# A quantised feed-forward whose up product runs on integers, with the token scale applied behind it

## The chip, the cores and the metric

The kernel runs on one core of a Trainium2 chip. The metric is the device time of one execution in microseconds (us). Three executions of the kernel before took 1745.68, 1744.78 and 1759.41 us; the median is 1745.68 us. Everything is computed in one launch. The engines are named as in the profile: PE is TensorE, DVE is VectorE, ACT is ScalarE, POOL is GpSimd, SP is the queue that only issues transfers.

## The reference

Eight sequences of 512 tokens with 512 features pass through four residual layers: cross attention with 16 heads, a mixture of experts, a second cross attention without projections, and a feed-forward with quantised operands. The change touches the last two layers only:

```python
def act_quant(x):
    scale = 127.0 / jnp.clip(jnp.max(jnp.abs(x), axis=-1, keepdims=True), 1e-05)
    return jnp.clip(jnp.round(x * scale), -128, 127) / scale
def weight_quant(w):
    scale = 1.0 / jnp.clip(jnp.mean(jnp.abs(w)), 1e-05)
    return jnp.clip(jnp.round(w * scale), -1, 1) / scale
...
h = bit_linear(x, w1)                       # act_quant(x) @ weight_quant(w1).T, 512 -> 2048
h = depthwise_conv1d(h.transpose(0, 2, 1), conv_w, conv_b)   # three taps along the tokens
h = jax.nn.silu(h.transpose(0, 2, 1))
return bit_linear(h, w2)                    # act_quant(h) @ weight_quant(w2).T, 2048 -> 512
```

The scale of `act_quant` is one number for each token (row), so it can be taken out of the matrix product and applied to its result.

## The kernel before

The program is four stages, one after the other: `attention`, `experts`, `fuse` and `ffn`. The first two end at about 1134 us of the profiled span and are not touched.

**fuse** handles the second attention. It runs in steps `s` from -1 to 8, a software pipeline over the eight sequences (batches, `B` = 8, `TB` = 4 tiles of 128 tokens each). In step `s`, `front` combines the expert outputs for batch s+1 into `x1`, `mid` runs the attention of batch s and writes `x3`, and `back` quantises batch s-1: ACT normalises into `xq`, DVE takes the row maximum `am`, ACT rounds by adding `MAGIC`, DVE multiplies back by the scale (`dequantise`, L1704), PE transposes (`out_transposes`, L1806), ACT copies to `xdT_out` (`copy_out`, L1641), and SP writes that to the scratch `xdT_d` (`store`). In its last steps the stage reads batch 0 back, and POOL splits it into a high and a low part (`first_parts`, L1603 and L1606), so that PE can compute the first four tiles of the feed-forward (`first_ups`, L1817) inside the stage.

**ffn** runs in steps `s` from -1 to 9. In step `s`, `f1` computes the 16 tiles `m` (128 hidden features by 512 tokens each) of batch s, `quant` finds and applies the token scales of batch s-1's hidden values, and `f2` is the down product of batch s-2. For one tile: `up(m)` on PE multiplies w1q with the two parts of `xdT` into one of four PSUM banks (`RING` = 4; L2145, eight matmuls); ACT writes the middle tap and the bias into the tile of `h` (L2009); DVE adds the two outer taps, reading the PSUM bank and `h` (`taps`, L2049 and L2052, signal `conv_done`); ACT applies SiLU (L1988). `half_max` (L2060) takes the maximum over eight tiles after m = 9 and over the other eight at the step's end; PE transposes the maxima (L2155), DVE makes scales of them (`token_scales`, L2065 to L2072), PE spreads them to a row (`scale_row`, L2161), ACT copies it to `srow` (L2002). Then POOL multiplies each tile of the batch before by `srow` (L1978), ACT rounds it (`lift_tile`, L1993) and PE takes it into the down product one step later (`down`, L2121 and L2123). The batch after next is fetched by SP and split by ACT (`high`, L1996) and DVE (`low`, L2076). The order on each engine is the order of the code; the engines meet by semaphores alone. POOL sums the second weight over its tiles into `wsum` at the stage's start (L1965 to L1971).

## Time and profile before

The profiled execution took 1753.9 us, of which its trace spans 1752.4 us from the first to the last instruction.

| | us |
|---|---|
| median of the three executions | 1745.68 |
| the profiled execution | 1753.9 |
| its span | 1752.4 |
| PE busy in the span | 1550.8 (88%) |
| DVE busy | 1060.4 (61%) |
| ACT busy | 791.9 (45%) |
| POOL busy | 622.9 (36%) |
| stage fuse, about | 1134 to 1334 |
| stage ffn, about | 1335 to 1752 |

A row of the timeline gives a start, a duration, the engine, the line of the kernel, what is written and read, and the count; in brackets stands how long the engine had been idle and what released it. The busy time of a group is the union of its instructions, which overlap in their fill and drain, so busy time divided by the count is nearer to the pace of a run of them than the mean duration is. An engine's instructions run in order; a semaphore wait holds everything behind it on that engine.

### The profile page before, as it was taken

Reading aid. Unit: us, or ns where it says so; the run is one execution under the profiler, and the core shown is the slowest. Engines: PE = TensorE matmul, PEld = TensorE weight load, DVE = VectorE, ACT = ScalarE, POOL = GpSimd, SP = SyncE. Lnnn points to the kernel's source line nnn. Section 1 sums busy time; section 2 is a strip of 40 time slices with the busy share of each in tenths; the row PEclk is TensorE's granted clock in tenths of the full one; section 3 lists DMA queues with packets and bytes.
Section 4 is the critical chain, followed back from the end, with each engine's and each line's share of the span. In section 5 each row is a group of like instructions: output and inputs, shape, how many; then the busy total and the mean of one; then the engine's idle time right before and its main releaser. Section 6 shows DMA issues by size and latency. Waiting matters only on the chain. (4 is left out here: it accounts for less than half of the span.)

```text
span 1752.4 us, 24975 instructions
## 1 busy us (share of the span) xinstructions
PE 1550.8 (88%) x8934; PEld 1218.5 (70%) x8956; DVE 1060.4 (61%) x1763; ACT 791.9 (45%) x1412; POOL 622.9 (36%) x584
## 2 busy tenths in 40 slices
PE   6599999999889999889999999567877789999997
PEld 5478878888668888767788888445556666666673
DVE  3468878788455553422233333269975877877775
ACT  2155555555321211113333444246666666766763
POOL 0134444444314666242412000265523443334440
PEclk9799999999899999999999999867678899999999
DMA  3123444333349999625533333598743112211202
GB/s 135 54 90 134 151 145 151 123 137 136 103 156 375 345 337 360 253 86 172 174 108 108 108 108 108 165 328 270 254 142 106 48 49 72 73 50 47 74 23 97
DMA packets 121334, 260.90 MB, mean 149 GB/s; under 512 B 15843, under 2 KB 24035, under 8 KB 119320
## 3 DMA queue, kind: packets, MB, share of 16 engines
q1 hardware_dynamic: 86440, 155.54, 26.6%
q0 software_dynamic: 17056, 67.12, 10.4%
q10 hardware_dynamic: 17744, 36.97, 5.6%
q8 instruction: 61, 1.00, 0.2%
q14 instruction: 33, 0.27, 0.0%
HBM read 147.13 MB, written 110.36 MB: 147 GB/s over the span
## 5 line engine op out<-in xcount | busy, mean ns | idle before, releaser
L2145 PE MATMUL f_banks<-xdT,w1q 128*128 128x512 f32 x992 | 239.6, 400 | 8.0 <-DVE b_h L2052 8.0
L2145 PEld LDWEIGHTS f_banks<-xdT,w1q 128*128 128x128 f32 x992 | 188.9, 192 | 49.4 <-DVE b_h L2052 9.1
L1978 POOL TENSOR_TENSOR b_h<-b_h,b_srow 128x512 f32<-128x512 f32 x112 | 143.4, 1327 | 205.5 <-ACT b_srow L2002 205.5
L202 PE MATMUL e_u_ps<-e_xs,w_shared 128*128 128x512 f32 x768 | 177.7, 392 | 6.1 <-DVE e_sg L1181 6.0
L202 PEld LDWEIGHTS e_u_ps<-e_xs,w_shared 128*128 128x128 f32 x768 | 145.0, 189 | 36.5 <-DVE e_sg L1181 6.1
L2009 ACT ACTIVATE b_h<-f_banks,cb,cw 128x512 f32<-128x512 f32 x128 | 104.6, 818 | 97.0 <-PE f_banks L2145 95.7
L2049 DVE SCALAR_TENSOR_TENSOR b_h<-f_banks,cw,b_h 128x511 f32<-128x511 f32 x128 | 95.7, 748 | 78.2 <-ACT b_h L2009 78.0
L1344 PE MATMUL e_u_ps<-e_w,e_xs 128*128 128x512 f32 x528 | 133.3, 401 | 2.0 <-DVE e_xs L1273 1.2
L1344 PEld LDWEIGHTS e_u_ps<-e_w,e_xs 128*128 128x128 f32 x528 | 95.9, 188 | 23.1 <-DVE e_xs L1273 1.6
L1281 DVE TENSOR_TENSOR e_hT<-e_r_ps,e_hT 128x256 fp32r<-128x256 f32 x69 | 29.2, 424 | 130.6 <-ACT e_hT L1121 130.6
L2123 PE MATMUL b_o_ps<-w2q,b_h 128*128 128x512 bf16 x441 | 102.9, 388 | 2.8 <-ACT b_h L1993 1.5
L806 PE MATMUL m_ps<-xT,wq 128*128 128x256 f32 x768 | 100.8, 289 | 1.4 <-DVE xT L625 1.4
L1988 ACT ACTIVATE b_h<-b_h 128x512 f32<-128x512 f32 x128 | 87.1, 681 | 29.7 <-DVE b_h L2052 29.6
L2052 DVE SCALAR_TENSOR_TENSOR b_h<-f_banks,cw,b_h 128x511 f32<-128x511 f32 x128 | 96.2, 752 | 4.5
L1328 PE MATMUL e_y_ps<-w_shared,e_hT 128*128 128x512 f32 x384 | 92.6, 402 | 6.9 <-DVE e_hT L1187 6.9
L1082 ACT ACTIVATE e_sg<-e_u_ps 128x512 f32<-128x512 f32 x32 | 19.0, 598 | 175.4 <-PE e_u_ps L202 172.2
L806 PEld LDWEIGHTS m_ps<-xT,wq 128*128 128x128 f32 x768 | 95.2, 194 | 1.8 <-DVE xT L625 1.8
L779 PE MATMUL m_ps<-wo,oT 128*128 128x512 f32 x384 | 96.0, 406 | 0.4 <-DVE oT L666 0.4
L544 POOL TENSOR_TENSOR xres<-xres,bo_t 128x512 f32<-128x512 f32 x32 | 40.6, 1289 | 150.7 <-DMA xres<-in_x 150.7
L569 ACT ACTIVATE pT<-t_ps 77x512 f32<-77x512 f32 x128 | 69.0, 589 | 51.3 <-PE t_ps L729 51.3
L1328 PEld LDWEIGHTS e_y_ps<-w_shared,e_hT 128*128 128x128 f32 x384 | 74.8, 195 | 23.5 <-DVE e_hT L1187 7.6
L779 PEld LDWEIGHTS m_ps<-wo,oT 128*128 128x128 f32 x384 | 72.4, 192 | 23.8 <-issue 6.6
(236 smaller groups left out, 3152.8 us busy)
## 6 DMA issues: line engine op xcount, KB each, us to landing
e_xe<-slots_in_scratch SPq DMA_DIRECT2D x69, 256.0 KB, 2.6
experts_out_scratch<-e_ye ACTq DMA_DIRECT2D x69, 256.0 KB, 2.0
xin<-in_x SPq DMA_DIRECT2D x16, 512.0 KB, 4.4
xres<-in_x SPq DMA_DIRECT2D x16, 512.0 KB, 5.3
x_scratch<-x SPq DMA_DIRECT2D x32, 256.0 KB, 2.0
xn_scratch<-xn SPq DMA_DIRECT2D x32, 256.0 KB, 2.0
xn2T_scratch<-x2T SPq DMA_DIRECT2D x16, 512.0 KB, 4.4
e_x<-x_scratch SPq DMA_DIRECT2D x32, 256.0 KB, 5.4
```

The source lines that it names most:

```text
L202: mm = pe.matmul(n.u_ps[:, (2 * q + j) % 4], n.w_shared[q // n.KH][:, pa, at:at + P], xs[:, pb, k], start=(k == 0 and (pa, pb) == PASSES[0 ...
L779: mm = pe.matmul(m_bank(*u), oT[:, pa, k, j * P:(j + 1) * P], wo[:, pb, k, :], start=(k == 0 and (pa, pb) == PASSES[0]), stop=(k == KD - 1 ...
L806: mm = pe.matmul(m_bank(*u)[:, g * W2:(g + 1) * W2], wq[:, pa, k, mt * P:(mt + 1) * P], xT[:, pb, k, :], start=(k == 0 and (pa, pb) == PAS ...
L1328: mm = pe.matmul(y_ps[:, t % 2], hT[:, pa, q, j * P:(j + 1) * P], w[e][:, pb, at:at + D], start=(q == 0 and (pa, pb) == PASSES[0]), stop=( ...
L1344: mm = pe.matmul(u_ps[:, 0], xeT[:, pa, k], w[par][:, pb, k * 2 * HID:(k + 1) * 2 * HID], start=(k == 0 and (pa, pb) == PASSES[0]), stop=( ...
L1978: pool.tensor_tensor(ht, ht, srow[:], ALU.mult).then_inc(u_done, 1)
L1988: act.activation(ht, ht, ACT.Silu).then_inc(h_done, 1)
L2009: act.activation(tile(s, m), f_ps[:, (s * KF + m) % RING], ACT.Identity, bias=cb[:, m:m + 1], scale=cw[:, m, 1:2]).then_inc(mid_tap, 1)
L2049: dve.scalar_tensor_tensor(out=ht[:, 1:S], in0=f[:, 0:S - 1], scalar=cw[:, m, 0:1], in1=ht[:, 1:S], op0=ALU.mult, op1=ALU.add).then_inc(pr ...
L2052: dve.scalar_tensor_tensor(out=ht[:, 0:S - 1], in0=f[:, 1:S], scalar=cw[:, m, 2:3], in1=ht[:, 0:S - 1], op0=ALU.mult, op1=ALU.add).then_in ...
L2123: mm = pe.matmul(o_ps[:, j % 2], rounded(s - 2, k, j), w2q[:, k, :], start=False, stop=(k == KF - 1))
L2145: mm = pe.matmul(f_ps[:, u % RING], w1q[:, k, m * P:(m + 1) * P], xdT[:, part, k], start=(k == 0 and part == 0), stop=(k == KD - 1 and par ...
```

## The change

The scale of the first quantisation moves behind the up product. fuse no longer multiplies back: PE transposes the rounded integers straight from the low halves of `xq` as 16-bit numbers, ACT takes the offset off and keeps all eight batches in SBUF as bf16 (`xqT`, and their scales in `dqa`), and the scratch in memory, its loads and the split into parts go away. The up product is one pass of four matmuls on bf16. Its result must then be multiplied by a row of token scales (`xrow`) before the taps, into a new SBUF ring `u` of six tiles. Of the 16 tiles of a batch, ten are evicted by ACT (`evict`) and scaled in place by POOL, six are scaled by DVE straight out of PSUM (`BY_VECTOR`). The taps read `u` where they read PSUM. POOL's products with `srow` are dealt out over m = 4 to 15 in between. The row maximum is taken over twelve tiles after m = 13 and over four at the step's end. The down product is cut into quarters, one after each `up`. The sum of the second weight moves from ffn's start into steps 6 and 7 of fuse.

```diff
-        n.w1q = keep("w1q", [P, KD, DH], FR)
+        n.w1q = keep("w1q", [P, KD, DH], BF16)
         n.w2q = keep("w2q", [P, KF, D], BF16)
-        n.xdT = keep("xdT", [P, 2, KD, S], FR)
-        n.xd = keep("xd_T", [P, KD, S], F32)
-        n.xdT_out = keep("xdT_out", [P, KD, S], F32)
+        n.xqT = keep("xqT", [P, B, KD, S], BF16)
+        n.dqa = keep("dqa", [P, NT], F32)
+        n.wsum = keep("wsum", [P, D], BF16)
+        n.lift = keep("lift", [P, P], BF16)
...
+            def weight_sum(step):
+
+                width = 8 >> step
+                if step == 0:
+                    pool.wait_ge(fw_in, 32)
+                    a, b = n.w2q[:, 0:8], n.w2q[:, 8:16]
+                else:
+                    pool.wait_ge(wsum_steps, step)
+                    a, b = part[:, 0:width], part[:, width:2 * width]
+                pool.tensor_tensor(part[:, 0:width] if step < 3 else n.wsum[:].rearrange("p (o d) -> p o d", o=1),
+                                   a, b, ALU.add).then_inc(wsum_steps, 1)
 
             def run(s, back, mid, front, par):
+                if s == B - 2:
+                    weight_sum(0)
+                    weight_sum(1)
...
-                if isinstance(s, int) and s == B - 1:
-                    first_parts()
+                if s == B - 1:
+                    weight_sum(2)
+                    weight_sum(3)
...
-                if j == 0 and not (isinstance(b, int) and b == 0):
-                    act.wait_ge(xd_out, b * 16)
                 act.wait_ge(dT_full, b * TB + j + 1)
-                act.activation(xdT_out[:, :, j * P:(j + 1) * P], d_ps[:, j % 2], ACT.Copy).then_inc(dT_copied, 1)
+                dst = n.xqT[:, ds(b, 1), :, j * P:(j + 1) * P].rearrange("p o k t -> p (o k) t")
+                act.activation(dst, d_ps[:, j % 2], ACT.Copy, bias=-OFFSET).then_inc(dT_copied, 1)
...
-                        if back:
-                            dequantise(s, j)
...
-                    mm = pe.transpose(d_ps[:, j % 2, k], xd[:, j, k * P:(k + 1) * P], ident[:])
+                    mm = pe.matmul(d_ps[:, j % 2, k], low_half[:, par, j, k * P:(k + 1) * P, 0], ident_h[:], start=True, stop=True)
...
+    UB = 6
     HB = 3
-    OFFSET = 1536.0
-    ROUND = MAGIC + float(0x6600)
+    AHEAD = 3
+    BY_VECTOR = (1, 4, 7, 9, 12, 15)
+    BY_POOL = tuple(m for m in range(KF) if m not in BY_VECTOR)
...
+        products = {4: (0, 1), 5: (2,), 6: (3, 4), 7: (5,), 8: (6,), 9: (7, 8), 10: (9,), 11: (10,), 12: (11, 12),
+                    13: (13,), 14: (14,), 15: (15,)}
+        lifts = {5: (0, 1), 6: (2,), 7: (3,), 8: (4, 5), 9: (6,), 10: (7, 8), 11: (9,), 12: (10,), 13: (11, 12),
+                 14: (13,), 15: (14,)}
...
-            part = x3[:, 1].bitcast(BF16).rearrange("p j (e d) -> p (j e) d", d=D)
-
-            pool.memset(lift[:], -OFFSET)
-            pool.tensor_tensor(part[:, 0:8], w2q[:, 0:8], w2q[:, 8:16], ALU.add).then_inc(wsum_steps, 1)
-            pool.wait_ge(wsum_steps, 1)
-            pool.tensor_tensor(part[:, 0:4], part[:, 0:4], part[:, 4:8], ALU.add).then_inc(wsum_steps, 1)
-            pool.wait_ge(wsum_steps, 2)
-            pool.tensor_tensor(part[:, 0:2], part[:, 0:2], part[:, 2:4], ALU.add).then_inc(wsum_steps, 1)
-            pool.wait_ge(wsum_steps, 3)
-            pool.tensor_tensor(wsum[:], part[:, 0], part[:, 1], ALU.add).then_inc(wsum_steps, 1)
+            def token_scale(v):
+                if v < B * KF and v % KF in BY_POOL:
+                    if v % KF == BY_POOL[0]:
+                        pool.wait_ge(xrow_done, v // KF + 1)
+                    pool.wait_ge(evicted, count(v, BY_POOL))
+                    pool.tensor_tensor(u[:, v % UB], u[:, v % UB], xrow[:, v // KF % 2], ALU.mult).then_inc(scaled_pool, 1)
+
+            def product(b, m):
+                if m == 0:
+                    pool.wait_ge(row_done, b + 1)
+                ht = tile(b, m)
+                pool.tensor_tensor(ht, ht, srow[:], ALU.mult).then_inc(u_done, 1)
 
             def run(s, f1, quant, f2, front):
-                if quant and f1:
-                    pool.wait_ge(row_done, s)
+                if f1:
                     for m in range(KF):
-                        ht = tile(s - 1, m)
-                        pool.tensor_tensor(ht, ht, srow[:], ALU.mult).then_inc(u_done, 1)
-
+                        token_scale(s * KF + m + AHEAD)
+                        if quant:
+                            for k in products.get(m, ()):
+                                product(s - 1, k)
+
+            for v in range(AHEAD):
+                token_scale(v)
             whole(run)(pool)
 
         @block.scalar
         def _(act):
+            def evict(v):
+                if v < B * KF and v % KF in BY_POOL:
+                    act.wait_ge(f_full, v + 1)
+                    if v >= UB:
+                        act.wait_ge(conv_done, v + 1 - UB)
+                    act.activation(u[:, v % UB], f_ps[:, v % RING], ACT.Copy).then_inc(evicted, 1)
...
+                        v = s * KF + m
+                        evict(v + AHEAD)
+                        wait_scaled(act, v)
+                        act.activation(tile(s, m), u[:, v % UB], ACT.Identity, bias=cb[:, m:m + 1],
                                        scale=cw[:, m, 1:2]).then_inc(mid_tap, 1)
+                        if m == 0 and s >= 2:
+                            lift_tile(s - 2, KF - 1)
                         if m >= 1:
                             silu(m - 1)
-                        if quant and m == 2:
-                            scale_row()
+                        if m == 3:
+                            if quant:
+                                scale_row()
+                            if front:
+                                token_row()
...
+            def token_scale(v):
+                if v < B * KF and v % KF in BY_VECTOR:
+                    if v % KF == BY_VECTOR[0]:
+                        dve.wait_ge(xrow_done, v // KF + 1)
+                    dve.wait_ge(f_full, v + 1)
+                    if v >= UB:
+                        dve.wait_ge(conv_done, v + 1 - UB)
+                    dve.tensor_tensor(u[:, v % UB], f_ps[:, v % RING], xrow[:, v // KF % 2], ALU.mult).then_inc(scaled_dve, 1)
...
-                    f, ht = f_ps[:, u % RING], tile(s, m)
-                    dve.wait_ge(mid_tap, u + 1)
+                    v = s * KF + m
+                    f, ht = u[:, v % UB], tile(s, m)
...
+                def part_max(i):
+                    first, last = (0, KF * 3 // 4) if i == 0 else (KF * 3 // 4, KF)
+                    dve.wait_ge(h_done, s * KF + last)
...
+                        token_scale(s * KF + m + AHEAD - 1)
                         taps(m)
-                        if m == 9:
-                            half_max(0)
-                        if f2 and m in (6, 12):
-                            outputs(2 + (m - 6) // 6)
+                        if quant and m == 0:
+                            token_scales()
+                        if m == 13:
+                            part_max(0)
+                        if f2 and m in (4, 8, 12):
+                            outputs(s - 2, m // 4 - 1)
+                    part_max(1)
...
-                        for part in range(2):
-                            mm = pe.matmul(f_ps[:, u % RING], w1q[:, k, m * P:(m + 1) * P], xdT[:, part, k],
-                                           start=(k == 0 and part == 0), stop=(k == KD - 1 and part == 1))
+                        mm = pe.matmul(f_ps[:, v % RING], w1q[:, k, m * P:(m + 1) * P], n.xqT[:, s, k],
+                                       start=(k == 0), stop=(k == KD - 1))
...
+                        if f2:
+                            down(m // 4, m % 4)
+                        if quant and m == 2:
+                            max_transposes()
+                        if m == 3:
+                            if quant:
+                                scale_row()
+                            if front:
+                                token_row()
```

On POOL in ffn the 112 products stand in one run of rows in the kernel before; `b_h` is the hidden tile and `b_srow` the row of its scales:

```order
L1965 TENSOR_TENSOR b_x<-w2q 128x4096
L1967 TENSOR_TENSOR b_x<-b_x 128x2048
L1969 TENSOR_TENSOR b_x<-b_x 128x1024
L1971 TENSOR_TENSOR b_wsum<-b_x 128x512
L1978 TENSOR_TENSOR b_h<-b_h,b_srow 128x512 x112
```

In the changed kernel a step's products (L1969) are mixed with the scaling of the next tiles (L1963); this is the part of m = 4 to 10 of step 1:

```order
L1969 TENSOR_TENSOR b_h<-b_h,b_srow 128x512 x2
L1963 TENSOR_TENSOR b_u<-b_u,b_xrow 128x512
L1969 TENSOR_TENSOR b_h<-b_h,b_srow 128x512 x3
L1963 TENSOR_TENSOR b_u<-b_u,b_xrow 128x512
L1969 TENSOR_TENSOR b_h<-b_h,b_srow 128x512
L1963 TENSOR_TENSOR b_u<-b_u,b_xrow 128x512
L1969 TENSOR_TENSOR b_h<-b_h,b_srow 128x512 x3
L1963 TENSOR_TENSOR b_u<-b_u,b_xrow 128x512
L1969 TENSOR_TENSOR b_h<-b_h,b_srow 128x512
```

So POOL now stands in front of the taps of each tile as well as behind them, with 26 instructions in a step where there were 16.

On DVE at the end of a step and the start of the next, before (L2060 the maximum, L2065 to L2072 the scales):

```order
L2049 SCALAR_TENSOR_TENSOR b_h<-f_banks,cw,b_h 128x511
L2052 SCALAR_TENSOR_TENSOR b_h<-f_banks,cw,b_h 128x511
L2076 TENSOR_TENSOR xdT<-xd_T,xdT 128x512
L2060 TENSOR_REDUCE b_am<-b_h 128x512
L2076 TENSOR_TENSOR xdT<-xd_T,xdT 128x512 x3
L2042 SCALAR_TENSOR_TENSOR b_x<-b_o_ps,b_d,b_x 128x512 x2
L2065 TENSOR_REDUCE b_mx<-b_q_ps 128x4
```

and in the changed kernel, from tile 15:

```order
L2056 TENSOR_TENSOR b_u<-f_banks,b_xrow 128x512
L2070 SCALAR_TENSOR_TENSOR b_h<-b_u,cw,b_h 128x511
L2073 SCALAR_TENSOR_TENSOR b_h<-b_u,cw,b_h 128x511
L2082 TENSOR_REDUCE b_am<-b_h 128x512
L2062 SCALAR_TENSOR_TENSOR b_x<-b_o_ps,b_d,b_x 128x512
L2070 SCALAR_TENSOR_TENSOR b_h<-b_u,cw,b_h 128x511
L2073 SCALAR_TENSOR_TENSOR b_h<-b_u,cw,b_h 128x511
L2087 TENSOR_REDUCE b_mx<-b_q_ps 128x4
```

The four low parts are gone, the first taps of the next batch stand between the maximum and the scales, and both inputs of the taps (`b_u`, `b_h`) now lie in SBUF.

On POOL in fuse, from the last instruction of step 5 to that of step 7, the changed kernel has (before, the four L1598 were not there, and a split of batch 0 stood in step 7):

```order
L1585 TENSOR_TENSOR f_ve<-f_mv,f_eps 128x4
L1587 TENSOR_TENSOR f_rs<-f_ve,f_half 128x4
L1598 TENSOR_TENSOR f_part<-w2q 128x4096
L1598 TENSOR_TENSOR f_part<-f_part 128x2048
L1585 TENSOR_TENSOR f_ve<-f_mv,f_eps 128x4
L1587 TENSOR_TENSOR f_rs<-f_ve,f_half 128x4
L1585 TENSOR_TENSOR f_ve<-f_mv,f_eps 128x4
L1587 TENSOR_TENSOR f_rs<-f_ve,f_half 128x4
L1598 TENSOR_TENSOR f_part<-f_part 128x1024
L1598 TENSOR_TENSOR wsum<-f_part 128x512
```

The two largest additions stand in front of the statistics of step 6, the two small ones in front of those of step 7.

## Rows read from the trace of the kernel before

**Rows 1.** Stretches: us, busy (x) of PE, PEld, DVE, ACT, POOL; clock; DMA, GB/s.
```profile
1575.00:1624.70 49.70, 45.99 (x209) 32.88 (x212) 38.87 (x48) 32.81 (x54) 20.50 (x16) 1.00 0.19 63
1335.00:1374.00 39.00, 26.46 (x105) 21.33 (x105) 34.61 (x38) 25.53 (x37) 15.63 (x5) 0.82 0.17 54
1168.70:1274.10 105.40, 84.28 (x371) 56.15 (x370) 96.68 (x237) 71.12 (x143) 57.06 (x67) 0.71 0.78 273
```

**Rows 2.** The chain that ended last, two steps of ffn: start, us, what.
```profile
1574.87 1.16 PE b_q_ps L2161 x8
...
1624.71 1.16 PE b_q_ps L2161 x8
```

**Rows 3.** Who waited for whom in fuse and ffn: total, times, longest.
```profile
POOL b_h L1978 <- ACT b_srow L2002: 205.5, 7, 32.8
ACT b_h L2009 <- PE f_banks L2145: 95.7, 49, 8.6
```

**Rows 4.** Groups of instructions in fuse and ffn by line and shape.
```profile
L2145 PE MATMUL f_banks<-xdT,w1q 128*128 128x512 f32 x992 | 239.6, 400 | 8.0 <-DVE b_h L2052 8.0
L2123 PE MATMUL b_o_ps<-w2q,b_h 128*128 128x512 bf16 x441 | 102.9, 388 | 2.8 <-ACT b_h L1993 1.5 <-issue 0.2
L2060 DVE TENSOR_REDUCE b_am<-b_h 128x512 f32<-128x4096 f32 x16 | 70.6, 4415 | 3.0 <-ACT b_h L1988 3.0
L2076 DVE TENSOR_TENSOR xdT<-xd_T,xdT 128x512 fp32r<-128x512 f32 x28 | 18.0, 682 | 0.0
L1641 ACT ACTIVATE xdT_out<-f_d_ps 128x512 f32<-128x512 f32 x32 | 17.4, 590 | 18.9 <-DMA xdT_scratch<-xdT_out 12.7 <-PE f_d_ps L1806 6.1
L1704 DVE TENSOR_SCALAR xd<-xq,dq 128x512 f32<-128x512 f32 x32 | 17.7, 553 | 1.2 <-ACT xq L1673 0.9
L1965 POOL TENSOR_TENSOR b_x<-w2q 128x4096 bf16<-128x4096 bf16 x1 | 8.0, 8021 | 0.0
L1967 POOL TENSOR_TENSOR b_x<-b_x 128x2048 bf16<-128x2048 bf16 x1 | 4.1, 4120 | 0.1
```

**Rows 5.** One step of ffn in order of time.
```profile
1575.50 0.75 DVE L2052 SCALAR_TENSOR_TENSOR b_h<-f_banks,cw,b_h 128x511 f32<-128x511 f32 x1
...
1576.94 0.75 DVE L2052 SCALAR_TENSOR_TENSOR b_h<-f_banks,cw,b_h 128x511 f32<-128x511 f32 x1
...
1579.83 20.50 POOL L1978 TENSOR_TENSOR b_h<-b_h,b_srow 128x512 f32<-128x512 f32 x16 [29.41 <-ACT b_srow L2002]
```

**Rows 6.** DVE and POOL in the expert stage, and line 1187's instructions (min/median/max ns).
```profile
713.30 9.76 DVE L1187 TENSOR_TENSOR e_hT<-e_sg,e_hT 128x512 fp32r<-128x512 f32 x2
...
712.65 2.75 POOL L1009 CAST e_w<-e_wraw 128x3072 fp32r<-128x3072 f32 x1 [9.61 <-DMA e_wraw<-in_w2e]
715.49 7.02 POOL L1011 TENSOR_TENSOR e_w<-e_wraw,e_w 128x3072 fp32r<-128x3072 f32 x1
...
L1187 DVE TENSOR_TENSOR e_hT<-e_sg,e_hT x32: 679/681/7187, 504.0 to 754.5; 128x512 fp32r<-128x512 f32 x32
```

**Rows 7.** DVE and POOL late in fuse; line 1606's first two (min/median/max ns).
```profile
1308.98 1.48 DVE L1704 TENSOR_SCALAR xd<-xq,dq 128x512 f32<-128x512 f32 x1
...
1307.49 5.31 POOL L1606 TENSOR_TENSOR xdT<-xd_T,xdT 128x512 fp32r<-128x512 f32 x4
...
L1606 POOL TENSOR_TENSOR xdT<-xd_T,xdT x2: 1270/1360/1449, 1307.5 to 1308.9; 128x512 fp32r<-128x512 f32 x2
```

**Rows 8.** The start of step 6 of fuse on DVE and POOL.
```profile
1274.09 2.74 DVE L1709 SCALAR_TENSOR_TENSOR y<-y,gcol,f_x 128x512 f32<-128x512 f32 x4 [0.30 <-DVE gcol L1746]
...
1274.02 1.01 POOL L1598 TENSOR_TENSOR f_rs<-f_ve,f_half 128x4 f32<-128x4 f32 x1
```

**Rows 9.** The end of fuse, in order of time.
```profile
1315.41 0.16 DVE L1753 SCALAR_TENSOR_TENSOR nmr<-f_mv,f_rs 128x4 f32<-128x4 f32 x1 [1.40 <-POOL f_rs L1598]
...
1319.15 1.08 ACT L1641 ACTIVATE xdT_out<-f_d_ps 128x512 f32<-128x512 f32 x2 [9.77 <-DMA xdT_scratch<-xdT_out]
...
1332.92 1.08 ACT L1641 ACTIVATE xdT_out<-f_d_ps 128x512 f32<-128x512 f32 x2 [0.32 <-PE f_d_ps L1806]
```

263 lines of the change are left out of this document (113 added, 150 removed).

## The prediction

> **What bounds the kernel now.** I read the stretches first, then the chain of waits, then the waits by pair. In a steady step of ffn PE is busy 46.0 of 49.7 us at a granted clock of 1.00, DVE 38.9, ACT 32.8, POOL 20.5 [rows 1]. The chain passes the same place every 49.84 us (1574.87 to 1624.71) [rows 2]. ACT waits 95.7 us in all for PE's up product, 49 times, and POOL waits 205.5 us for the row of scales, so POOL has more than half of each step to itself [rows 3]. So seven of ffn's eight `f1` steps (s = 1 to 7) are bound by PE; step 0 takes 39.0 us with DVE busy 34.6 of it [rows 1]. fuse is different: over five of its steps DVE is busy 96.7 of 105.4 us, so 21.1 us a step are DVE's, with PE's clock at 0.71 [rows 1].
>
> **The change on each engine, in one steady step of ffn.** PE loses 64 of 128 up matmuls. One costs 239.6/992 = 0.242 us at the pace of the run, and the bf16 ones of the down product 102.9/441 = 0.233 us, so the type brings nothing and the count does [rows 4]: 46.0 - 64 x 0.242 = 30.5, plus about 1.2 for the row of token scales (as long as the one in [rows 2]) = 31.7 us. DVE loses four low parts (18.0/28 = 0.64 each) and gains six scalings at the same price: 38.9 - 2.6 + 3.8 = 40.1. ACT gains ten evictions at 17.4/32 = 0.54 and a row, less its four splits: at most 38.8 [rows 1, 4]. POOL goes from 16 to 26 instructions at 20.5/16 = 1.28: 33.3 us [rows 5]. By these sums alone DVE would bound a step at about 41 us.
>
> **What the sums leave out.** Before, the taps read one input from PSUM and one from SBUF, and their pace is 1.44 us a tile (1575.50 to 1576.94) [rows 5]. After, both inputs lie in SBUF, and POOL reads SBUF nearly all the time. The nearest rows are in the expert stage. L1187 is a DVE operation of 128x512 with both inputs in SBUF; its median is 0.681 us. At 713.30 two of them take 9.76 us, and the longer takes 7.187: POOL's cast runs to 715.40, its product from 715.49 to 722.51, and the DVE pair ends at 723.06 [rows 6]. DVE stood still for the whole of POOL's instruction and finished 0.55 after it. The reverse price is small: late in fuse POOL's products last 1.270 alone and 1.449 with a DVE operation let in between [rows 7], so DVE's turn costs POOL 0.18, because much of it lies in POOL's own start. A DVE operation and a POOL operation that take turns hence need 1.27 + 0.18 + a little = 1.48 us a pair. The bounds: 1.28 if DVE's turn is free, 1.28 + 0.72 = 2.00 if nothing overlaps. I take 1.48, which is nearest to the rows.
>
> The Trainium skill, "SBUF — State Buffer", section "Who interferes with whom", says that a DVE instruction with two SBUF inputs contends with a GpSimd instruction that reads SBUF, as an exclusive lock for the whole instruction. It speaks against this change; the 7.187 us above agree with it. Read strictly it would make a pair 2.00 us, and the third rival below is that case; the 0.18 us of [rows 7] disagree with so strict a reading.
>
> **A steady step, tile by tile.** (a) m = 4 to 12: POOL has exactly two instructions a tile, 18, and DVE 18 taps. In turns: 18 x 1.48 = 26.6 us. DVE's scalings and outputs read PSUM on one side and fit into POOL's turns. Two of POOL's may lag and end under the maxima, so I take 16 x 1.48 + 2 x 0.72 = 25.1. (b) m = 13 to 15: three tiles 4.3, two scalings 1.3, and the maximum over twelve tiles, 4.42 x 1.5 = 6.6 [rows 4], under which POOL works off five of its instructions: 12.2. (c) SiLU of the last tile and the maximum over four, 0.8 + 2.2 = 3.0; the sum of the two maxima is what it was. (d) m = 0 to 3: four tiles 5.8, an output 0.7, a scaling 0.7, the scales 1.75, and about 1.9 in which ACT waits for the row and DVE for ACT: 10.8. Sum 51.1; with 0.4 for a PE that stands still for some 13 us around the maxima and comes back at the lower clock, 51.5. Against 49.84 that is +1.65 a step, +11.5 for seven. What PE gives back (14 us a step) is hidden by this: PE is late nowhere, DVE is.
>
> **The rest of ffn.** The stage begins with PE's row, its copy, an eviction and a POOL scaling before the first middle tap: about 1.2 + 0.6 + 0.5 + 1.3 with their handovers = +4. Step 0: ten POOL scalings among the taps and six on DVE, less the low parts: 16 tiles at 2.0 + 9.5 = 41.5 against 39.0 [rows 1], +2.5. In step 8 the row of scales now stands behind one more down product of 16 matmuls (16 x 0.233 = 3.7 us), while DVE needs 1.75 for the scales: +1.5.
>
> **fuse.** In the middle steps DVE loses `dequantise`, four a step at up to 17.7/32 = 0.55 [rows 4], 2.2 in all, but in the loop that it stood in DVE also waits for PE, which only loses part of its transposes. Between nothing and 2.2 I take 1.0 a step for seven, -7. The end: `nmr` of the last batch is ready at 1315.4, but ACT waits 9.77 us for the store of `xdT_out` and its last copy ends at 1334.0 [rows 9]. Without that store the wait goes, and with the first ups halved PE is free when the last transposes come; I take 0.8 for that: -10.6. The loads and stores of `xdT` cost nothing by themselves elsewhere, as SP has nothing urgent behind them.
>
> The sum of the second weight cost nothing before: it ran (8.0 and 4.1 us [rows 4]) under taps that read PSUM. Now POOL starts it at 1275.03, right behind the statistics of step 5, while DVE's four combinations, both inputs in SBUF, run from 1274.09 to 1276.83 [rows 8]. By [rows 6] the third waits for the 8.0 us and the fourth for the 4.1 us that follow: DVE reaches 1288.3 instead of 1276.8, +11.5, and DVE is the bound there. In step 7 the two small sums (2.1 and 1.1, halving on from 4.1) meet `nmr`, +2.5. If the taking of turns does not hold, both are nothing.
>
> **The sum.** -7 - 10.6 + 11.5 + 2.5 + 4 + 2.5 + 11.5 + 1.5 = +15.9 us. The profiled execution of 1753.9 becomes 1769.8; it lay 8.2 above the median of the three (1745.68), so the median becomes about 1761. Less than 1% (17 us) is about what a measurement of this kernel cannot tell from no change.
>
> **Rivals.** *First, on the other side: the taps do not wait for POOL.* For it: the unmoved 0.75 us of the taps under POOL's products, though these read PSUM [rows 5]. Against: [rows 6]. Then (a) is 18 x 1.28 = 23.0, POOL's own pace, and (d) about 1 less, a step 47.3 or better 46.5 as POOL may lag into the maximum: -3.4 x 7 = -24; the weight sums are free (-14 against my sum), step 0 gives -1. In all -7 - 10.6 + 4 - 1 - 24 + 1.5 = -37, that is 1709. It decides from a pair below 1.3 us. *Second, in between: turns are taken, but many of POOL's instructions fall into DVE's waits for ACT, its outputs and scalings.* A step of 48 us gives 15.9 - 7 x 3.5 = -8.6, 1737. *Third, nothing overlaps:* pairs of 2.00 make (a) 32 to 36 and a step 59: +52 on top, 1814. *Fourth, the loop closes:* POOL's scaling of tile m+3 stands behind products that wait for the row, ACT's middle tap behind the scaling, the taps behind ACT, and PE comes back at half clock (1.2 of 2.4 GHz; granted clocks of 0.71 and 0.82 stand in [rows 1] where PE has gaps), where a tile's eight matmuls take twice 1.9 us. A step of 54 gives 1779. *Fifth, the change does not do what it says:* PE's half could be spent on weight loads; the down product's pace speaks against it, under 2 in 100.
>
> **How the numbers follow.** My case (1750 to 1773) 0.35; first rival 0.15; second 0.22; third 0.08; fourth with the fifth 0.20. The predicted time is that of my case, 1761. The range from 1710 to 1790 leaves out the third rival and half of the first; my case alone has 1750 to 1773. Faster by over 1% (below 1728): the first and half of the second, 0.26. Within 1% (to 1763): half of the second and over half of mine, 0.33. Slower: 0.41.
>
> **What would show it.** In the changed profile: taps of 0.75 us only where POOL stands still, and of 1.2 to 1.5 us elsewhere, a mean above 1.0; a combination of 7 to 8 us in step 6 of fuse; steps of ffn between 50 and 53 us with DVE the engine that never idles; PE busy near 32 us a step; no wait for `xdT_scratch` and an end of fuse 10 us shorter. A mean of the taps of 0.75 would make the prediction wrong towards 1709; steps above 53 us with DVE waiting for ACT, towards 1779.

## The result, and the profile of the changed kernel

The changed kernel takes 1912.94 us (median of 4 runs, 1911.38 to 1915.75) against 1748.59 us for the kernel before (the three runs known at the forecast and one more, 1744.78 to 1759.41): a ratio of 1.093, interval 1.088 to 1.098. The forecast was 1761 in a range of 1710 to 1790, so the sign of the single value was right and its size was wrong by 152 us. The profiled execution has a span of 1914.3 us (before 1752.4) at a granted clock of 0.878.

The page's busy times and two of its slice rows (each slice 47.9 us):

```profile
PE 1506.5 (79%) x8508; PEld 1100.5 (57%) x8508; DVE 1198.1 (63%) x1751; ACT 828.9 (43%) x1472; POOL 768.1 (40%) x657
...
DVE  3578888885555442223333337995887787787785
...
PEclk9699999999899999999999977666677788788778
```

PE does 426 matmuls fewer than before (8508 for 8934) but is busy only 44 us less (1506.5 for 1550.8). In ffn, the last twelve slices, its clock stays at 6 to 8 tenths; DVE's digits are 7 and 8, and 5 in the last slice.

The same stretch as in [rows 1], one steady step from one transpose of the maxima to the next; and the start and length of the transposes on the chain of waits, first and last of the seven steps and two between:

```profile
1662.63:1734.29 71.66, 42.10 (x157) 20.03 (x157) 57.02 (x50) 37.59 (x60) 40.09 (x26) 0.81 0.09 30
```
```profile
1378.94 1.97 PE b_q_ps L2172 x8
...
1662.63 1.97 PE b_q_ps L2172 x8
...
1734.29 1.97 PE b_q_ps L2172 x8
...
1876.99 1.97 PE b_q_ps L2172 x8
```

For the kernel before the same two places stand at 1372.26 on the chain and, in its order of time, here:

```profile
1719.55 1.04 PE L2155 MATMUL b_q_ps<-ident,b_am 128*128 128x128 f32 x8
```

So seven steps take 498.05 us for 347.29, 71.2 us each for 49.6. That is +150.8 of the +161.9 us between the two spans. DVE is busy 57.0 us a step, not 40, and it is also idle 14.6 us a step.

The groups of instructions that answer to [rows 4] and [rows 5] (busy us, mean ns, idle before them):

```profile
L2070 DVE SCALAR_TENSOR_TENSOR b_h<-b_u,cw,b_h 128x511 f32<-128x511 f32 x128 | 153.3, 1198 | 73.2 <-ACT b_h L2020 72.5
L1969 POOL TENSOR_TENSOR b_h<-b_h,b_srow 128x512 f32<-128x512 f32 x112 | 182.4, 1649 | 12.8 <-ACT b_srow L2007 12.8
...
L2161 PE MATMUL f_banks<-xqT,w1q 128*128 128x512 bf16 x496 | 156.5, 455 | 23.0 <-DVE b_u L2056 23.0
L2073 DVE SCALAR_TENSOR_TENSOR b_h<-b_u,cw,b_h 128x511 f32<-128x511 f32 x128 | 165.4, 1292 | 4.5
...
L2138 PE MATMUL b_o_ps<-w2q,b_h 128*128 128x512 bf16 x448 | 143.7, 454 | 15.9 <-ACT b_h L2001 15.9
```

Each tap takes 1.20 and 1.29 us on the mean for 0.75. An up matmul costs 156.5/496 = 0.316 us for 0.242, a down matmul 143.7/448 = 0.321 for 0.233: halving the ups saved PE 83 us, and 41 went back into downs that are slower at the lower clock.

The waits (who for whom, total us, times, longest) that the forecast did not have:

```profile
ACT b_u L1990 <- PE f_banks L2161: 124.4, 31, 8.4
...
PE b_o_ps L2135 <- DVE b_x L2062: 98.4, 18, 7.4
```

ACT's evictions wait 124 us for up products, though PE has a great deal of time to spare, and PE waits 98 us for DVE's outputs. Each of DVE, ACT and PE waits for another. The chain of waits at the start of the step shows how:

```profile
1660.29 2.30 DVE b_am L2082
1662.59 0.04 issue
1662.63 1.97 PE b_q_ps L2172 x8
1664.60 1.72 PE f_banks L2161 x4
...
1666.39 0.60 ACT b_u L1990
1666.99 0.75 ACT b_h L2020
...
1667.76 1.14 DVE b_h L2070
...
1671.35 0.10 DVE b_s L2094
1671.45 0.04 issue
1671.49 3.56 PE b_q_ps L2177 x16
1675.05 0.86 PE f_banks L2161 x4
```

PE executes in order. The transposes of the maxima stand in front of the up product of tile 3; they wait for DVE's second maximum, so ACT's eviction of tile 3 waits for both, ACT's middle tap of tile 0 stands behind that eviction in ACT's program, and DVE waits 4.53 us for it. Nine microseconds later the same happens again: up(4) stands behind the row of scales and the row of token scales.

### The profile page after: what moved, and what is told of

The parts are those of the page before. It is cut to its first block and busy times, and to the rows that moved or that the text cites. A ratio compares the mean times of both kernels' runs of the same rounds, so it can differ in the third digit from the quotient of the medians.

```text
span 1914.3 us, 24289 instructions
## 1 busy us (share of the span) xinstructions
PE 1506.5 (79%) x8508; PEld 1100.5 (57%) x8508; DVE 1198.1 (63%) x1751; ACT 828.9 (43%) x1472; POOL 768.1 (40%) x657
## 5 line engine op out<-in xcount | busy, mean ns | idle before, releaser
L1963 POOL TENSOR_TENSOR b_u<-b_u,b_xrow 128x512 f32<-128x512 f32 x80 | 116.5, 1458 | 234.5 <-ACT b_u L1990 234.5
L2070 DVE SCALAR_TENSOR_TENSOR b_h<-b_u,cw,b_h 128x511 f32<-128x511 f32 x128 | 153.3, 1198 | 73.2 <-ACT b_h L2020 72.5
L1969 POOL TENSOR_TENSOR b_h<-b_h,b_srow 128x512 f32<-128x512 f32 x112 | 182.4, 1649 | 12.8 <-ACT b_srow L2007 12.8
L2161 PE MATMUL f_banks<-xqT,w1q 128*128 128x512 bf16 x496 | 156.5, 455 | 23.0 <-DVE b_u L2056 23.0
L2073 DVE SCALAR_TENSOR_TENSOR b_h<-b_u,cw,b_h 128x511 f32<-128x511 f32 x128 | 165.4, 1292 | 4.5
L2138 PE MATMUL b_o_ps<-w2q,b_h 128*128 128x512 bf16 x448 | 143.7, 454 | 15.9 <-ACT b_h L2001 15.9
L2161 PEld LDWEIGHTS f_banks<-xqT,w1q 128*128 128x128 bf16 x496 | 56.0, 114 | 101.5 <-issue 36.2
L2020 ACT ACTIVATE b_h<-b_u,cb,cw 128x512 f32<-128x512 f32 x128 | 108.9, 853 | 0.5 <-POOL b_u L1963 0.5
L2138 PEld LDWEIGHTS b_o_ps<-w2q,b_h 128*128 128x128 f16 x448 | 55.7, 124 | 90.0 <-issue 30.2
L1990 ACT ACTIVATE b_u<-f_banks 128x512 f32<-128x512 f32 x80 | 47.1, 592 | 124.4 <-PE f_banks L2161 124.4
```

The lines of the kernel that those rows point to most:

```text
L1963: pool.tensor_tensor(u[:, v % UB], u[:, v % UB], xrow[:, v // KF % 2], ALU.mult).then_inc(scaled_pool, 1)
L1969: pool.tensor_tensor(ht, ht, srow[:], ALU.mult).then_inc(u_done, 1)
L2020: act.activation(tile(s, m), u[:, v % UB], ACT.Identity, bias=cb[:, m:m + 1], scale=cw[:, m, 1:2]).then_inc(mid_tap, 1)
L2070: dve.scalar_tensor_tensor(out=ht[:, 1:S], in0=f[:, 0:S - 1], scalar=cw[:, m, 0:1], in1=ht[:, 1:S], op0=ALU.mult, op1=ALU.add).then_inc(pr ...
L2073: dve.scalar_tensor_tensor(out=ht[:, 0:S - 1], in0=f[:, 1:S], scalar=cw[:, m, 2:3], in1=ht[:, 0:S - 1], op0=ALU.mult, op1=ALU.add).then_in ...
L2138: mm = pe.matmul(o_ps[:, j % 2], rounded(s - 2, k, j), w2q[:, k, :], start=False, stop=(k == KF - 1))
```

## The experiments

The theory after this reading had two parts. **Turns:** a DVE tap with both inputs in SBUF and a POOL instruction exclude each other, and a pair costs more than the 1.48 us I took. **PE's order:** where PE waits for DVE (maxima, scales, outputs), up products that ACT and DVE need soon stand behind the wait. The rivals: only one of the two; or PE's low clock as a cause in itself. The kernels of one run each are compared by their ffn steps, since the whole of the same kernel moves by more than 10 us from one execution to the next (the kernel before: 1740.9 to 1759.4 us). "A step" is the mean of the seven between transposes of the maxima where nothing else is said.

### Turns alone, in the kernel before

```
-                    f, ht = f_ps[:, u % RING], tile(s, m)
+                    f, ht = stand, tile(s, m)
```

> The kernel before, with one edit: the first tap of every tile reads a constant SBUF tile (all ones) instead of the PSUM bank, so DVE's tap has both inputs in SBUF as in the changed kernel; PE, ACT and POOL have the same work and order as before (the result of the convolution is no longer the reference's). Theory A (DVE and POOL take turns, 1.70 us for a pair): the taps (L2123) that lie beside POOL's 16 products of a step go from 0.75 to 1.2-1.8 us, POOL's products from 1.28 to 1.4-1.7, a step grows from 49.8 to 52-58 us, ffn by 20-60 us. Theory B (the taps' source is harmless, the +22 us a step of the changed kernel come from PE's order and its clock): taps stay at 0.75 us, the time within 10 us of before.

1812.5 us, beside 1753.2 for the kernel before. The edit gives both taps of a tile the constant tile `stand`, not the first alone. From one scale row to the next the steps take 55.9 us for 49.85. Groups, and one step in order of time:

```profile
L2054 DVE SCALAR_TENSOR_TENSOR b_h<-b_stand,cw,b_h 128x511 f32<-128x511 f32 x128 | 150.2, 1174 | 33.5 <-ACT b_h L2012 33.3
...
L1981 POOL TENSOR_TENSOR b_h<-b_h,b_srow 128x512 f32<-128x512 f32 x112 | 189.2, 1727 | 216.9 <-ACT b_srow L2005 216.9
```
```profile
1562.41 0.75 DVE L2057 SCALAR_TENSOR_TENSOR b_h<-b_stand,cw,b_h 128x511 f32<-128x511 f32 x1
...
1566.54 1.79 DVE L2054 SCALAR_TENSOR_TENSOR b_h<-b_stand,cw,b_h 128x511 f32<-128x511 f32 x1
1568.36 1.68 DVE L2057 SCALAR_TENSOR_TENSOR b_h<-b_stand,cw,b_h 128x511 f32<-128x511 f32 x1
```
```profile
1562.69 27.05 POOL L1981 TENSOR_TENSOR b_h<-b_h,b_srow 128x512 f32<-128x512 f32 x16 [28.85 <-ACT b_srow L2005]
```

The tap that starts before POOL does, at 1562.69, takes 0.75 us; from 1564.92 on nearly every tap takes 1.7 to 1.8, and the sixteen products take 27.05 us instead of 20.50 [rows 5]. Apart from the filling of `stand` nothing but the source of the taps differs, so this is shown: the second SBUF input causes turns. The six taps from 1566.54 to 1576.87 follow each other every 1.72 us, which is the price of a pair; 27.05/16 = 1.69 is the mean of all sixteen products, the last of which lie beside DVE's maximum and take no turns.

> As the run before it (taps' first input from a constant SBUF tile), and POOL's 16 products of a step work on 8 of 512 columns (left out: the other 504 columns of the scaling), so POOL touches SBUF for very little time. Theory A: taps are back at 0.75 us and the time at that of before or a little below (1730-1755). Theory B: no difference to the run with full products.

> The kernel before, only POOL's products on 8 of 512 columns (left out: the other 504 columns of the scaling); the taps read PSUM as before. It is the baseline for the two runs with the constant tile. Both theories: the time of before or up to 10 us less, taps 0.75 us.

```
-    pool.tensor_tensor(ht, ht, srow[:], ALU.mult)
+    pool.tensor_tensor(ht[:, 0:8], ht[:, 0:8], srow[:, 0:8], ALU.mult)
```

1755.3 and 1756.1 us. With POOL out of the way the constant tile costs nothing: the steady steps are 49.8 and 49.8 us (over all seven 49.4 and 49.4, before 49.6), and the first tap is

```profile
L2054 DVE SCALAR_TENSOR_TENSOR b_h<-b_stand,cw,b_h 128x511 f32<-128x511 f32 x128 | 106.0, 828 | 73.5 <-ACT b_h L2012 73.5
```

0.83 us on the mean for 0.75; what is left may be short turns with the narrow products. POOL's own work is not what bounds the kernel before: narrow, it changes nothing (1756.1 us is 3 above 1753.2, which is less than executions differ).

### Turns and order in the changed kernel

Two edits, alone and together, and a third on top. POOL narrow is the edit above on both of POOL's operations. The order of PE:

```
                         if s or m >= RING:
                             up(m)
+                        if quant and m == 4:
+                            max_transposes()
                         if f2:
                             down(m // 4, m % 4)
-                        if quant and m == 2:
-                            max_transposes()
-                        if m == 3:
+                        if m == (5 if quant else 3):
```

and the outputs on DVE two tiles earlier:

```
-                        if f2 and m in (4, 8, 12):
-                            outputs(s - 2, m // 4 - 1)
+                        if f2 and m in (2, 6, 10):
+                            outputs(s - 2, m // 4)
```

> The changed kernel, with both of POOL's operations in ffn (the ten token scalings and the sixteen products of a step) on 8 of 512 columns (left out: the other 504 columns); order, waits and all other work are the changed kernel's. Theory A alone (turns between DVE and POOL are all that is wrong): a step falls from 71.7 to 41-45 us (DVE's own busy time of about 40 us), the whole to 1690-1710. Theory B alone (PE's order and clock): a step stays above 65, the whole above 1860. Theory C (both: the turns stretch DVE and POOL, and PE's in-order waits for the maxima, the scales and the outputs add the rest): a step of 48-60 us, the whole 1730-1830, with DVE still idle 5 to 12 us a step and the taps at 0.75.

> The changed kernel with PE's order alone altered: the transposes of the maxima stand behind the up product of tile 4 instead of behind tile 2's down product, and the row of scales with the row of token scales behind tile 5's down product instead of tile 3's, so that two or three more up products can run before PE stops for DVE's second maximum. Nothing is left out. In the changed kernel DVE stood 4.5 and 2.6 us of such a place for ACT's middle tap, which stood for an up product behind those two waits, and a scaling 3.1 us. Theory C (turns plus PE's order): a step falls from 71.7 to 62-67 us, the whole from 1913 to 1840-1880. Theory A (turns alone): PE's order matters little, since the row of scales now comes later for POOL: 1900-1930.

> The altered PE order and POOL's operations of ffn on 8 of 512 columns (left out: the other 504 columns of the token scalings and the products). The same kernel with PE's order as changed gave 1830 us. Theory C: DVE's 106 us of waits for ACT's middle tap in ffn (13 a step) shrink to under 50, a step falls from 61 to 50-56 us, the whole to 1760-1800. Theory D (PE's low clock is a cause in itself, whatever the order): a step stays at 58-61 us, the whole above 1815.

> The altered PE order, and DVE takes each output two tiles earlier (behind tiles 2, 6, 10 instead of 4, 8, 12), so that the next down product, which needs the freed bank, does not hold the up products behind it on PE. PE waited 98 us in all for such outputs, 18 times, in the changed kernel. Nothing is left out. Theory C: 2 to 4 us a step less than with PE's order alone, the whole 15 to 30 us below that run. Theory A: within 8 us of it. If the outputs then make DVE itself wait for the down product at that place, it is slower.

> The altered PE order with the outputs two tiles earlier, and POOL's operations of ffn on 8 of 512 columns (left out: the other 504 columns of the token scalings and the products). It completes the table of both causes: steps measured so far are 71.7 (neither mended), 61.0 (POOL narrow), 64.9 (PE's order), 51.0 (both), 59.9 (PE's order and the outputs). If the waits for the outputs are a separate cost of PE's order, they are worth 3 to 5 us here too: a step of 46 to 48 us, the whole 1720 to 1745. If they only mattered because DVE was slowed by turns, a step stays at 50 to 51 us and the whole within 8 us of 1762.

The whole and the mean step, in us:

| | POOL as changed | POOL on 8 columns |
|---|---|---|
| PE's order as changed | 1912.9, step 71.2 | 1830.1, step 59.5 |
| PE's order altered | 1858.3, step 63.4 | 1762.4, step 50.2 |
| and the outputs earlier | 1832.2, step 59.4 | 1737.2, step 47.2 |

(The expectations name steady steps alone, which are up to 1.5 us longer.) Going right saves 11.6, 13.3 and 12.2 us in the three rows: POOL's full width costs about 12 us a step whatever PE's order. Going down saves 7.7 and 4.1 on the left, 9.4 and 3.0 on the right: PE's order, with the place of the outputs, costs about 12 us a step whatever POOL does. The causes add up, which neither "turns alone" nor "order alone" allows: 47.2 + 12 + 12 = 71. The whole of each of the five came out within what the theory of both causes expected, that of the narrow kernel at the very end of its range (1830). Not everything did: in the narrow kernel DVE is idle 20.1 us a step where 5 to 12 were expected, its steady steps go up to 62.5 us where 60 was the limit, and with PE's order altered DVE's waits for the middle tap fell from 106 to 57 us, not under 50, and the earlier outputs gave 4.1 us at full width where 2 to 4 were expected.

Narrowing POOL takes away the turns and POOL's own work together, so the 12 us of the columns alone do not tell which of the two it was. DVE's busy time does: it is 56.6, 56.5 and 56.2 us a step down the left column and 39.8, 39.7 and 39.7 down the right. Stretched taps cost DVE 16.7 us a step, of which some 12 reach the step, as DVE then waits less. With order and outputs mended and POOL at full width DVE is busy 56.2 of 59.4 us: there its stretched taps are the bound, and not a POOL that comes late.

The last expectation's choice is settled too: the waits for the outputs are a cost of their own, 3.0 us without turns (its range was 46 to 48 for the step, and 1720 to 1745 for the whole). One step of the narrow kernel, and one of the one with everything mended, as stretches:

```profile
1612.28:1672.75 60.47, 37.76 (x153) 19.38 (x156) 40.41 (x50) 36.53 (x60) 5.58 (x26) 0.84 0.10 35
```
```profile
1511.71:1559.48 47.77, 33.99 (x155) 17.26 (x157) 40.22 (x50) 36.27 (x60) 5.92 (x26) 0.89 0.13 44
```

DVE's busy time is nearly the same in both, 40.4 and 40.2 us; 12.5 of the 12.7 us between them are its idle time. In the first, over the whole of ffn,

```profile
DVE b_h L2070 <- ACT b_h L2020: 106.0, 78, 5.1
```

with next to no turns (the taps are at 0.75 us again): that is PE's order, and these waits fall to 57 us where it is altered.

### Is it the clock?

> The changed kernel, and PE makes each up product twice in a row (the second overwrites the first), so PE has the number of up matmuls of the kernel before; result and everything else unchanged. Theory D (the 22 us a step come from PE's low clock, which sits at 0.81 because PE has too little to do): the clock comes back to 0.95 to 1.00 in ffn and a step is 71.7 us or less. Theory C (PE's order and the closed loop): the second pass stands in the path wherever others wait for an up product, so a step grows by 3 to 10 us, 75 to 82 us, the whole 1935 to 1990, whatever the clock.

```
+                    for part in range(2):
                         for k in range(KD):
```

1945.1 us, and a steady step:

```profile
1672.64:1747.49 74.85, 51.19 (x216) 25.15 (x221) 57.40 (x50) 38.03 (x60) 39.56 (x26) 0.89 0.08 29
```

PE's busy time goes from 42 to 51 us and the clock from 0.81 to 0.89 in this step (0.79 to 0.89 over the six behind the first), but these steps are 75 to 82 us long. More work for PE brings the clock back a little and the time not at all. The clock did not reach 1.00 as that theory asked, so this run does not price a full clock.

Two kernels of the table bear on it as well. The seven steps of the changed kernel, then those with order and outputs mended and POOL at full width:

```profile
1378.94:1876.99 498.05, 284.38 (x1022) 132.93 (x1022) 396.19 (x338) 261.32 (x417) 279.57 (x180) 0.76 0.06 21
```
```profile
1378.95:1794.52 415.57, 253.65 (x995) 116.73 (x1014) 393.62 (x338) 260.38 (x414) 288.82 (x179) 0.79 0.07 26
```

The clock is nearly the same, 0.76 and 0.79, and the second takes 82.5 us less; 79.9 of these are DVE's idle time (101.9 us, then 22.0). So what stands in front of what in PE's queue is worth its 12 us a step while the clock stays low. And the kernel with everything mended takes 47.8 us a step at 0.89, less than the 49.8 of the kernel before at 1.00 [rows 1]. What the low clock adds by itself is not shown, as no run changes the clock alone. It is not nothing: the eight transposes at the start of the step take 1.97 us where the row of the kernel before has 1.04, and the up product behind them 1.72 where the next takes 0.86, and all of these lie in the chain above.

### The sums of the second weight in fuse

```
-                    a, b = n.w2q[:, 0:8], n.w2q[:, 8:16]
+                    a, b = n.w2q[:, 0:8, 0:8], n.w2q[:, 8:16, 0:8]
```

(and the three smaller sums likewise; what they no longer write is set to zero once at the start of fuse)

> The changed kernel with the four sums of the second weight in fuse on 8 of 512 columns each (left out: the other 504 columns of these sums); ffn is unchanged. Theory (each long POOL instruction that reads SBUF stops DVE's combinations and sums for its whole length): fuse's step 6 is 11.5 us shorter and step 7 some 2.5 us, the whole 12 to 15 us below the changed kernel's 1913. Rival (fuse's DVE catches up later, at the wait for the last products): within 4 us of it.

1905.3 us, which is 7.6 less where 12 to 15 were expected; as single executions differ by more than that, the whole says little. In the traces the distance from the first combination to the row of token scales, which starts ffn, is 1147.4 to 1330.2 = 182.8 us in the changed kernel and 1149.6 to 1320.5 = 170.9 here: 12 us. Step 6 on DVE and POOL, changed kernel, then this one:

```profile
1269.52 14.19 DVE L1701 SCALAR_TENSOR_TENSOR y<-y,gcol,f_x 128x512 f32<-128x512 f32 x4 [0.30 <-DVE gcol L1738]
...
1270.43 8.28 POOL L1598 TENSOR_TENSOR f_part<-w2q 128x4096 bf16<-128x4096 bf16 x1
1278.78 4.37 POOL L1598 TENSOR_TENSOR f_part<-f_part 128x2048 bf16<-128x2048 bf16 x1
```
```profile
1271.78 2.79 DVE L1703 SCALAR_TENSOR_TENSOR y<-y,gcol,f_x 128x512 f32<-128x512 f32 x4 [0.30 <-DVE gcol L1740]
```

Four combinations take 14.19 us beside the sums and 2.79 without: DVE stands for nearly the whole of both. The Trainium skill, "SBUF — State Buffer", section "Who interferes with whom", has this as an exclusive lock held for the whole instruction; the trace agrees: POOL's second sum ends at 1283.15 and the combinations at 1283.71, 0.56 us later.

### A kernel without either cause

DVE scales every tile in place in its PSUM bank, so the middle tap and the taps read the bank again and have one SBUF input; the evictions, `u` and POOL's ten scalings are gone, and the sums of the weight stand beside step 0 of ffn as before. PE transposes the maxima behind up(3) and makes the scale row behind tile 4; the outputs stand behind tiles 3, 7 and 11.

```
+            def token_scale(v):
+                if v < B * KF:
+                    if v % KF == 0:
+                        dve.wait_ge(xrow_done, v // KF + 1)
+                    dve.wait_ge(f_full, v + 1)
+                    dve.tensor_tensor(f_ps[:, v % RING], f_ps[:, v % RING], xrow[:, v // KF % 2], ALU.mult).then_inc(scaled, 1)
...
-                    f, ht = u[:, v % UB], tile(s, m)
+                    f, ht = f_ps[:, v % RING], tile(s, m)
```

> A version meant to keep the one pass and lose both causes: DVE scales every tile in place in its PSUM bank (16 times 0.68 us a step), ACT's middle tap and DVE's taps read the bank again (one SBUF input), POOL has only the 16 products, no evictions, the sums of the second weight stand in ffn beside step 0 as before, maxima transposed behind the up product of tile 3, scale row behind tile 4, outputs taken behind tiles 3, 7, 11. Whole computation. By DVE's instructions a step is 24.0 (taps) + 10.9 (scalings) + 8.8 (maxima) + 3.0 (outputs) + 1.8 (scales) = 48.5 us, PE 32 to 38. If turns and order were the whole cause: steps of 49 to 51 us (before 49.85), taps at 0.75, fuse about 14 us shorter than before, the whole 1730 to 1750, within 1% of before or faster. If the integer path has another cost (PE's clock below 0.9 alone): steps of 54 us or more, the whole above 1770.

1718.01 us against 1749.88 for the kernel before (medians of 4 and 7 runs): a ratio of 0.983, interval 0.979 to 0.987. It is faster than the kernel before by a little under 2%, and than the changed kernel by 10%. As several things change together, it shows what a kernel without the two costs can do, and not the price of either. A step:

```profile
1525.32:1572.00 46.68, 35.25 (x154) 16.16 (x156) 45.32 (x60) 32.15 (x51) 20.32 (x16) 0.93 0.13 46
```

DVE is busy 45.3 of 46.7 us: at last the bound that the forecast expected. It came out below what was expected, 49 to 51 and 1730 to 1750: the single durations add up to 48.5, but DVE's instructions overlap a little where they follow each other without a wait, and its busy time counts that once. fuse is 13.9 us shorter than before, for 14 expected. First taps are back at 0.743 us, with POOL's sixteen products at a pace of 1.27.

> The version that scales in place, and the outputs of six of the eight batches are scaled by ACT (0.59 us each) and added by POOL (1.3 to 1.5 us each) instead of by DVE (0.74 us). Whole computation. DVE is the bound of the version before it, so a step loses up to 3.0 us: 46 to 48 us, the whole 10 to 20 us below it, 1710 to 1735. If ACT's order is what bounds then (read in front of the middle tap), no gain or up to 10 us slower.

```
+  act.activation(y[:, j % 2], o_ps[:, j % 2], ACT.Copy, scale=d2[:, b % 2, j:j + 1]).then_inc(o_read, 1)
+  pool.tensor_tensor(x3[:, b % 2, j], x3[:, b % 2, j], y[:, j % 2], ALU.add).then_inc(o_added, 1)
```

1720.94 us, 0.982 (0.978 to 0.986): no different from the version before it, where 10 to 20 us less were expected. DVE is busy 42.9 us a step, but

```profile
1487.57:1533.46 45.89, 34.33 (x155) 15.94 (x156) 42.91 (x56) 34.23 (x55) 25.36 (x21) 0.93 0.13 46
```

the step falls only from 46.7 to 45.9. Of the 2.4 us taken from DVE 0.8 arrive; what takes the rest stays open. Over the seven steps that is 4 us, too little to be seen in the whole: in the two profiled executions the first combination of fuse, up to which the two kernels are the same, comes at 1140.5 and at 1148.5 us.

## Why the prediction was wrong

**The step, by its own four parts.** The forecast put them at 25.1, 12.2, 3.0 and 10.8 us, in all 51.1. The step from 1662.6 to 1734.2 measures, from DVE's instructions: (a) tiles 4 to 12, 1684.65 to 1717.20, 32.5; (b) tiles 13 to 15 with the first maximum, to 1731.2, 14.0; (c) 3.0; (d) tiles 0 to 3, 22.1. So (c) was exact, (b) 1.8 short (the two taps in front of the maximum still take turns), (a) 7.4 short and (d) 11.3 short.

**The price of a pair** is the step that failed in (a). I took 1.48 us, "nearest to the rows". POOL in the changed kernel, beside taps without a break:

```profile
1697.06 1.73 POOL L1963 TENSOR_TENSOR b_u<-b_u,b_xrow 128x512 f32<-128x512 f32 x1
1698.75 5.15 POOL L1969 TENSOR_TENSOR b_h<-b_h,b_srow 128x512 f32<-128x512 f32 x3
```

is four instructions in 6.84 us, 1.71 each, and the constant tile in the kernel before gave 1.72. The 0.18 that "DVE's turn costs POOL" came from [rows 7], where DVE's operation is L1704, 0.48 us long; a tap is 0.75, 0.27 longer, and 1.45 + 0.27 is 1.72. So the price had to be carried over with the length of DVE's instruction. That the length is what makes the difference is argued from these two pairs: L1704 is also of another kind, with one tile as input where a tap has two.

By 1.70 the 18 pairs of (a) are 30.6 us, 5.5 more than my 25.1; 3.5 of them are the price and 2.0 the two pairs that I let lag, which did not. The rest of the 32.5 is a wait:

```profile
1706.98 1.12 DVE L2070 SCALAR_TENSOR_TENSOR b_h<-b_u,cw,b_h 128x511 f32<-128x511 f32 x1 [1.93 <-ACT b_h L2020]
```

ACT's middle tap stood there behind an eviction, that one waited for an up product, and the up product stood on PE behind a wait of 4.95 us for DVE's output: PE's order again. The mechanism of turns, the place and the sign were right. The strict reading (2.00, the third rival) does not hold for pairs of this length: about 0.3 us of each pair overlap.

**"PE is late nowhere, DVE is"** is the step that failed in (d), where the larger part of the step's error lies. I set PE's sum of work (31.7 us) against the step and took PE as free, without following what stands behind its waits, tile by tile. The maxima come at the step's end, PE has up products for only three tiles in hand, and the change put its waits at tiles 2 and 3 in front of the products that ACT's three-tile lead needs. In the kernel before ACT's middle tap read the bank of its own tile; now the eviction of tile m+3, for the ten tiles that go by POOL, stands ahead of the middle tap of tile m, so ACT asks for tile 3 before it serves tile 0. The waits of DVE in (d):

```profile
1667.76 1.13 DVE L2070 SCALAR_TENSOR_TENSOR b_h<-b_u,cw,b_h 128x511 f32<-128x511 f32 x1 [4.53 <-ACT b_h L2020]
...
1675.95 0.69 DVE L2056 TENSOR_TENSOR b_u<-f_banks,b_xrow 128x512 f32<-128x512 f32 x1 [3.07 <-PE f_banks L2161]
1679.29 1.12 DVE L2070 SCALAR_TENSOR_TENSOR b_h<-b_u,cw,b_h 128x511 f32<-128x511 f32 x1 [2.64 <-ACT b_h L2020]
...
1684.65 0.75 DVE L2070 SCALAR_TENSOR_TENSOR b_h<-b_u,cw,b_h 128x511 f32<-128x511 f32 x1 [1.02 <-ACT b_h L2020]
```

They come to 11.3 us where I had 1.9, which is 9.4 of what (d) is short. The first three are PE's order; the last stands behind ACT's copies of the two rows, which I had counted. The remaining 1.9 are nearly all turns with POOL's scalings (taps of 1.13, 1.12 and 1.75 for 0.75). PE's order with the place of the outputs is worth 12 us a step by the table above.

**PE's 31.7 us** became 42.1, at a clock of 0.81 where the prices I used were taken at 1.00. I had "0.4 for a PE that stands still for some 13 us around the maxima". It stood still 9.7 us there, and 19.8 us more elsewhere in the step: 16.3 in three waits for DVE's outputs, of which the forecast had nothing, and 3.5 before the row of scales.

**The rivals.** The first (taps do not wait) did not come: its condition, pairs below 1.3 us, was not met. The kernel with POOL on 8 columns and PE's order mended takes 47.2 us a step, where that rival had 46.5 to 47.3, but this is luck: the rival had POOL's own pace of 1.28 as the limit of (a), and in that kernel POOL has next to nothing to do. Its sum does not come out either: 23.0 + 12.2 + 3.0 + 9.8 is 48.0, not 47.3. The fourth, a closed loop at 54 us, had the right kind of mechanism and the wrong link: it let POOL's scalings hold up ACT from behind POOL's products, and POOL's scaling kept ACT waiting once in all of ffn, for 0.5 us. It was priced at 2.5 us a step above my case (54 for 51.5), where the order costs about 12, and the range, to 1790, left no room for turns at their full price and stalls together.

**fuse.** The weight sums in step 6: +11.5 forecast, 14.19 - 2.74 = +11.45 measured; with step 7, 14 forecast and 12 measured. The end without the store: -10.6 forecast, and from the last combination to the last copy it went from 57.9 to 46.3 us with the sums narrow, -11.6; the wait for `xdT_scratch` is gone. The middle: 1.0 a step forecast for seven steps. In the five steps whose work is alike, from the second group of four combinations to the seventh, it was right. They take 104.9 us before (1169.23 to 1274.09) and 99.3 in the changed kernel (1170.25 to 1269.52), 1.1 us less each:

```profile
1169.23 2.74 DVE L1709 SCALAR_TENSOR_TENSOR y<-y,gcol,f_x 128x512 f32<-128x512 f32 x4
```
```profile
1170.25 2.74 DVE L1701 SCALAR_TENSOR_TENSOR y<-y,gcol,f_x 128x512 f32<-128x512 f32 x4
```

It holds in every other profile: 103.0 to 103.6 us in the three others with the fuse of before, 99.2 to 99.3 in all those of the changed fuse, so the gain is 0.7 to 1.1 us a step. The sum hides it, because the first step went from 17.4 to 22.9 us; that one varies with the execution (17.4 to 23.8 us over all the profiles, 21.6 to 22.8 in the other three with the fuse of before). In all fuse came to +0.3 for the forecast's -3.6: +5.5 for the first step, -5.6 for these five, +12 for the sums and -11.6 at the end.

**The rest of ffn.** Its start, last copy to first middle tap, went from 1.2 to 4.9 us: +3.7 for +4. Step 0, first middle tap to the transposes, 37.0 to 44.1: +7.0 for +2.5, with the same turns. What each part of it costs was not measured. Behind the last transposes 32.9 to 37.3: +4.5 for +1.5, and the cause of the 3 us between stays open.

**The sum.** -4.4 (the first combination comes that much earlier, ahead of the change) + 0.3 + 3.7 + 7.0 + 150.8 + 4.5 = 161.9, the difference of the spans. Without the -4.4 and the 150.8 the terms come to +15.5, and the forecast had +4.4 for them; the steady steps had +11.5. The error is in the steady step, 19.9 us seven times.

## What to carry to other kernels

When a change moves an operand from PSUM to SBUF for one engine's lighter load, look at every DVE instruction with two SBUF inputs beside POOL's work, and price a pair with DVE's own length in it: here it was POOL's time plus DVE's time less about 0.3 us. When an in-order engine gets light, its busy time says nothing about when its results come: list what stands behind each of its waits, and who needs that within the depth of the ring. The two costs added up here, so a range has to hold their sum.
